# A new hand-written order for everything behind attention in a four-layer kernel, with more idle products on TensorE

## What is computed

```
xn = _layernorm(x, axis=-1)
s = attention_l(xn)
g = _silu(ffn_l(xn))
x = x + s * g
```

## Time and profile before

| what | us |
|---|---|
| median of 3 runs | 993.38 (993.24 to 994.14) |
| the profiled execution | 993.47 |
| its span | 991.7 |
| PE busy, share of the span | 921.9, 93% |
| DVE busy, share of the span | 758.0, 76% |
| phase C begins on PE | 610.4 |

### The profile page before, as it was taken

The page is one execution under the profiler, slowest core; times in us unless marked ns, Lnnn a source line. Parts: engine busy times, 40 slices in busy tenths (PEclk is TensorE's granted clock), DMA queues, the critical chain, the costliest instruction groups (busy, mean ns, idle before and its releaser), DMA issues. The chain is left out here.

```text
span 991.7 us, 21236 instructions
## 1 busy us (share of the span) xinstructions
PE 921.9 (93%) x7847; PEld 496.3 (50%) x7847; DVE 758.0 (76%) x1329; ACT 538.3 (54%) x902; POOL 596.8 (60%) x533
## 2 busy tenths in 40 slices
PE   4899998999999999999999998799999888899997
PEld 2346563233333333333322333699888546488794
DVE  6878788888888888887888825983689999863414
ACT  1255346666676666666665785443266144275453
POOL 3660426888778777887777894124635787652333
PEclk9899999999999999999999999999999999999999
DMA  9463525111110201121011123567851200343562
GB/s 318 152 216 104 149 81 159 47 53 48 34 52 25 61 24 49 34 60 58 22 40 41 32 70 90 169 209 225 261 153 43 91 20 24 93 132 102 145 198 80
DMA packets 93749, 98.24 MB, mean 99 GB/s; under 512 B 23344, under 2 KB 69808, under 8 KB 93392
## 3 DMA queue, kind: packets, MB, share of 16 engines
q1 hardware_dynamic: 88528, 86.39, 28.6%
q0 software_dynamic: 5120, 10.50, 3.7%
HBM read 71.09 MB, written 25.30 MB: 97 GB/s over the span
## 5 line engine op out<-in xcount | busy, mean ns | idle before, releaser
L254 PE MATMUL ps<-ar 64*64 64x512 bf16 (+5 forms) x5312 | 532.8, 445 | 14.6 <-DVE small L276 4.9
L254 PEld LDWEIGHTS ps<-ar 64*64 64x64 bf16 (+2 forms) x5312 | 264.0, 136 | 268.0 <-ACT ar L300 88.6
L300 ACT ACTIVATE ar<-ps 128x1024 f32<-128x1024 f32 (+1 forms) x304 | 285.2, 941 | 112.0 <-PE ps L254 105.2
L276 DVE TENSOR_REDUCE small<-ps 128x2 f32<-128x1024 f32 (+2 forms) x276 | 307.2, 1140 | 50.5 <-PE ps L254 49.1
L263 POOL TENSOR_TENSOR psum_sb<-psum_sb,ar 128x1024 f32<-128x1024 f32 x91 | 215.0, 2362 | 57.3 <-DVE on_sb L263 47.0
L263 POOL TENSOR_TENSOR ar<-ar 128x512 f32<-128x512 f32 (+1 forms) x80 | 79.3, 997 | 47.3 <-DVE ar L276 26.1
L322 POOL DMA_INDIRECT gT<-ysort,rt x48 | 46.5, 968 | 99.6 <-issue 98.0
L263 DVE TENSOR_TENSOR ar<-ps,ar 128x256 f32<-128x256 f32 (+4 forms) x56 | 56.2, 1011 | 47.3 <-PE ps L254 46.2
L263 POOL TENSOR_TENSOR psum_sb<-ar 128x1024 f32<-128x1024 f32 x32 | 75.9, 2373 | 13.3 <-ACT ar L300 11.0
L297 ACT COPY ar<-ps 128x256 f32<-128x256 f32 (+1 forms) x84 | 31.6, 385 | 79.2 <-PE ps L254 48.2
L254 PE MATMUL ps<-wA,xnT 128*128 128x512 f32 (+3 forms) x192 | 57.9, 425 | 5.1 <-DVE ar L263 2.9
(11 more groups left out here) (159 smaller groups left out, 1089.4 us busy)
## 6 DMA issues: line engine op xcount, KB each, us to landing
ar<-in_L_up SPq DMA_DIRECT2D x48, 384.0 KB, 4.0
ar<-in_L_b SPq DMA_DIRECT2D x32, 322.0 KB, 3.4
rec_sb<-lscr SPq DMA_DIRECT2D x64, 128.0 KB
scr<-ar SPq DMA_DIRECT2D x48, 128.0 KB, 2.1
ar<-xsort SPq DMA_DIRECT2D x40, 128.0 KB, 4.3
ysort<-ar SPq DMA_DIRECT2D x40, 128.0 KB, 3.1
ar<-scr SPq DMA_DIRECT2D x32, 128.0 KB
xsort<-xs SPq DMA_DIRECT2D x12, 256.0 KB, 6.5
```

The source lines that it names most:

```text
L254: return self.e.matmul(o, l, r, start=start, stop=stop) if self.e else Nothing()
L276: return self.e.tensor_reduce(o, a, AX.X, op, negate=True) if negate else self.e.tensor_reduce(o, a, AX.X, op)
L300: return self.e.activation(o, a, fn, **kw) if self.e else Nothing()
```

## The change

Only the lists of words change. No stage is written anew, and each stage does the same work.

- `ORDER_A["tensor"]` gets five more words: `busy.6.0.50`, `busy.4.0.51`, `busy.4.0.52`, `busy.3.0.53` and `busy.4.0.54`, which are 21 idle products. The rest of that list stands as it stood.
- `ORDER_C` is replaced on all five engines. The words are the same and come equally often, in another order. Only the idle products differ: nine words with 67 products before, fourteen with 94 now. The order on SP comes from a plan in which its transfers share one line.

One line of the diff for A and the first one for C (the lists go on for some 80 lines):

```diff
-        "ln.0.0 ln.0.1 qk.0.0 route.0 v.7 v.5 v.7 ln.0.3 v.1 ln.0.2 route.0 route.1 v.3 v.11 v.5 qk.0.1 v.11 v.3 v.15 "
...
+        "ln.0.0 ln.0.1 qk.0.0 route.0 v.7 v.5 v.7 busy.6.0.50 ln.0.3 v.1 busy.4.0.51 ln.0.2 route.0 route.1 v.3 v.11 v.5 "
...
 ORDER_C = {
     "tensor": (
-        "tables tables tail0 tables tables tables xturn.2 up.2 xturn.2 up.2 end0.2 xturn.2 tail0 tail0 tail0 busy.9.5.0 "
...
+        "tables tables tables busy.14.5.0 tables tables tail0 tail0 xturn.2 xturn.2 up.2 up.2 up.2 xturn.2 up.2 end0.2 "
```

More of the change, by code:

```diff
@@ L148 @@
     "tensor": (
[24 rows of a table removed]
-    "vector": (
-        "tables position tables tail0 tables tables tables end0.2 tables tables tail0 tail0 tail0 end0.2 tables gated.2 "
[18 rows of a table removed]
-    "scalar": (
[17 rows of a table removed]
[25 rows of a table added]
+    "vector": (
+        "position tables tables tables tables tables tail0 gated.2 tail0 tail0 end0.2 gated.2 tables tables gated.2 "
[18 rows of a table added]
+    "scalar": (
[17 rows of a table added]
     "gpsimd": (
         "clear2 ln.1.2 ln.1.3 route.3 route.3 route.3 route.3 gather.2 gather.2 gather.2 gather.2 gather.2 gather.2 "
[6 rows of a table removed]
[6 rows of a table added]
         "gather.4 gather.4 gather.4 gather.4 gather.4 gather.4 gather.4 gather.5 gather.5 gather.5 gather.5 gather.5 "
```

## The result

The changed kernel takes 997.11 us in the median of 16 runs against 993.31 for the kernel before on the same chips: a ratio of 1.0040, 95% interval 1.0028 to 1.0051. The ratios are taken over all runs and not from the two medians, whose quotient is 1.0038; one run of `a_alone`, of 1080.02 us, is left out of its ratio as slow. It is slower by 0.4%, where 984.0 had been forecast. Its profiled execution took 996.48 us with a span of 994.7, which is 3.0 us more than the span of before.

What follows compares the result with a forecast made beforehand. It took PE as bound in layer 3's expert stage, DVE in the tile stage, and chains at the start behind attention and the end; -1.0 - 9.4 + 0.6 - 3.7 + 4.0 = -9.5 from 993.5 gave 984.0 us, range 978.4 to 994.0.

Steps and rivals of the forecast that it cites:

- Part 1: Idle products in A: they hold the clock up near 25 to 32 us and shorten DVE's wait, -1.0 us.
- Part 2: From attention to layer 2's first tile: real work fills PE's waits and two gathers move behind `ln.2.0`, -9.4 us.
- rival (a): Front: delayed softmax sum or SP's queue keeps PE waiting at `ln.1.3`; start gives little, 989.0 us; chance 0.17.
- The delay of `tail0`: Front: last softmax sum some 3 us later, hidden if `up.2` work fills the time until `ln.1.3`.
- Part 3: Tile stage: DVE sets the pace, PE's slack takes in its added work; only DVE's own growth counts, +0.6 us.
- rival (c): Tile stage: PE becomes the bound as idle products delay DVE, up to +11.8 us, total 995.2 or 997.8; chance 0.09.
- Part 4: First `up.4` to last `down.5`: PE is gapless, work leaving it is full gain, less 0.9 us new waits, -3.7 us.
- Part 5: Behind the last `down.5`: PE's chain with all of `att3.3` outlasts the gathers, +4.0 us, ends +1.2 and +7.0.
- the hand-overs: End of kernel: three passes from PE over DVE or ACT and back, 1.2 us each, 3.5 us in all.
- Rival (d): End of kernel: PE's tail runs at the low clock, 999.4 us if all of it, 989 if a third; chance 0.05.
- three signs of being wrong: First tile under 4 us early; DVE idle over 10 us in the tile stage; or gathers still ending last.

Runs made afterwards that it cites:

- a_alone: Kernel before with only the change's 21 idle products in A added: ratio 1.0018 to the kernel before.
- no_tile_products: Changed kernel without its 72 idle products behind the first tile: ratio 1.0078 to the kernel before.
- c_alone: Changed kernel with the old list in A, so without the 21 idle products there: ratio 1.0052 to the kernel before.
- front_new_a: Kernel before with the change's order from attention to the first tile and the change's idle products in A: ratio 0.9965 to the kernel before.
- front_warm_a: Kernel before with the change's order up to the first tile, eight more idle products in that front, and the change's products in A: ratio 0.9993.
- new_half_products: Changed kernel with half of each group of idle products behind the first tile: ratio 1.0041 to the kernel before.
- front_new: Kernel before with the change's order from attention to the first tile, old order behind it, old A: ratio 0.9968 to the kernel before.
- rec_moved: Changed kernel with one `rec.3` word of DVE's list moved behind the first words of `tile.6` and `tile.7`: ratio 1.0055 to the kernel before.
- x_mid_old: Changed kernel with the old order on all engines between `tile.0` and `tile.8`: ratio 1.0040 to the kernel before.
- new_from_up4: Kernel before with the change's order only from the first `up.4` on PE to the end: ratio 1.0035 to the kernel before.
- old_double_products: Kernel before with each idle product behind the first tile doubled, 72 in place of 36: ratio 1.0042 to the kernel before.

## Why the prediction was wrong, point by point

**Part 1** had -1.0 and got -0.9 ahead of phase C in the profiled execution. One execution of each could not have shown that: phase C begins at 607.9 to 614.3 in the nine kernels with the old A and at 606.9 to 609.7 in the eight with the new one, means 610.1 and 609.1. The clock did not stay up but fell later. It was low for 3.4 us in place of 6.8; with the old A this first fall took 3.4 us in six of nine kernels, and 6.8 or 13.7 in the others, with the new one 3.4 in all eight. The windows of the changed kernel that answer to the earlier trace rows:

```profile
25.00:32.00 7.00, 6.34 (x36) 0.87 0.24 102
32.00:40.00 8.00, 7.52 (x23) 0.90 0.58 182
```

The rule of the Trainium skill (TensorE: Matmul & The Clock Gate, section HAM oscillation — how this bites in real kernels), by which short bursts between waits throw the clock back, had been set aside because the waits of the earlier trace rows had left the clock at 1.00. It deserved more: the clock fell in the changed kernel at 30.2 and at 661.7, and in `no_tile_products` at 662.3, 795.4 and 836.3, the last two in the tile stage. But the trace agrees with that rule only in part. The case that the Trainium skill describes there is a wait for a transfer that is longer than the work ahead of it. Ahead of 661.7 the waits were of 0.65 and 0.84 us, and PE was busy for 2.51 of the 4.0 us around them.

At the end of the kernel nothing of the gain in A could be shown. In four pairs that differ in A alone, the ratio with its products is higher by 0.0018 (`a_alone`), lower by 0.0012 (the changed kernel against `c_alone`), lower by 0.0003 (`front_new_a`) and higher by 0.0039 (`front_warm_a`). They lie on both sides of nothing, so a term of -1.0 us (0.001) cannot be told from them. Only the last pair is clear of its intervals, and it is a loss whose cause is open.

**Part 2** had the direction and half the size. Up to the last `down.2` two terms failed. It came 79.6 us after the start of phase C, not 73.6: PE idled 4.8 us, not 3.0, and its work was 74.8 us in place of 70.6, since the sum had put a fall of the clock at nothing. `c_alone`, whose clock stayed up to there, has 71.7 us of work, 4.9 of idle time and 76.7 in all. With 3.4 us of low clock it is 78.2 to 78.3 in six kernels, with 6.8 it is 79.6 to 79.8 in four. So the fall is the larger term, about 3 us.

It was not what decided the first tile, though, and here the path of the sum was wrong too: gathers do not simply follow the last `down.2`. The first row of `gather.2` in POOL's timeline, in `c_alone`:

```profile
693.22 1.00 POOL L324 DMA_INDIRECT gT<-ysort,rt  x1 [13.23 <-issue]
```

and in the changed kernel:

```profile
692.90 1.00 POOL L323 DMA_INDIRECT gT<-ysort,rt  x1 [11.41 <-issue]
```

Counted from the start of phase C, `c_alone` ended `down.2` at 76.7 and began to gather at 85.3, the changed kernel at 79.6 and 83.5. Between the two stand the stores of the result rows. The last one ahead of the gathers was issued at 80.3 in `c_alone`, behind loads of rows and weights on SP, and landed at 84.5; in the changed kernel 80.1 and 82.8. In `new_half_products`, `down.2` ended at 78.3, a store issued at 79.0 landed at 85.4 and the gathers began at 86.5, and its first tile was the latest of all with the new front. So SP's line, which rival (a) had named for another transfer, has a part in this front; no run moved it alone, and its share is not shown. The delay of `tail0` that I had seen and taken for hidden was there: `ln.1.3` came 32.0 us after the start of phase C, 4.1 later than before. Behind `down.2` the sum was near in this execution: 29.7 us to the first tile where 30.5 follow from the forecast. The change wins 4.3 in the front, and `front_new` shows that this gain is real.

**Part 3** is the largest miss, 6.9 of 12.5 us; with the 5.1 of Part 2 it turned the sign, and neither would have done it alone. The step that failed: "As long as DVE sets the pace, PE's 18 us of slack take this in. I take +0.6". The slack did take the second half of the products in, as `new_half_products` showed. But DVE's own time was not what I had summed. I had taken the durations of before and DVE's idle time of before as given. From the first tile to the end of `route.4` it works 1.9 us more: 2.3 for the meeting with POOL at 777 us, 1.7 less at three places where it had met POOL before, and the rest for `gather.2`, `gated.3` and other words that crossed the borders of the stretch. It idles 2.2 us more, since other words wait in other places. And the list of PE puts 3.4 us more between `route.4` and the first `up.4`, which I had written down as work but not as delay. Two such waits in the changed kernel's DVE timeline, where it reaches a step of a tile and a `gated.3` before ACT has got to it:

```profile
762.73 0.42 DVE L277 TENSOR_REDUCE ar<-ar 128x16 f32<-128x256 f32 x1 [0.64 <-ACT ar L301]
...
764.53 0.55 DVE L264 TENSOR_TENSOR psum_sb<-ar,ps 128x384 f32<-128x384 f32 x1 [0.64 <-ACT ar L301]
```

So rival (c) had the place and 7.5 of its 11.8 us, but the wrong mechanism: it is the order of the real work on DVE and PE, and not the idle products. Which of the moved words makes DVE wait was not found: `rec_moved` and `x_mid_old` each took back a part of the order, and neither became faster.

**Part 4** predicted -3.7 and got -0.5. PE's work fell from 104.1 to 102.0 us, not to 99.3: `att3.3` and `ffn2.3` left, but the same instructions of `up.5`, `xturn.5` and `att3.1` took 1.3 us longer in their new places (most of it in products of the form `ps<-ar 128x128`), and waits of 1.9 us opened where 0.9 had been allowed. The other 1.4 us between 102.0 and 99.3 was not broken down. `new_from_up4`, with 103.6 us, has the same length without the new tile stage ahead of it, so it is this order that does not pay.

**Part 5** had the right mechanism and the dear end of the hand-overs. PE's last stretch in the changed kernel, which answers to the earlier trace rows:

```profile
973.75 1.88 PE L255 MATMUL ps<-xnT,wA 128*128 128x512 f32 x4
...
981.63 7.45 PE L255 MATMUL ps<-ar 128*128 128x512 f32 x22
989.76 0.66 PE L258 MATMUL ps<-cf,acc_sb 128*128 128x128 f32 x4 [0.68 <-ACT acc_sb L298]
```

PE was busy for 15.77 of its last 20.8 us, where I had 15.4 of work, and the only wait of a size was 0.68 us: the hand-overs that I had put at 3.5 were filled by other products of the block. So the end cost 1.3, close to my lower end of +1.2. Rival (d), the low clock in the tail, did not happen: the window's clock was 0.95 because it fell at 992.7, when PE had been done since 990.4.

The range from 978.4 to 994.0 did not hold 997.11, because its upper side rested on +0.6 for Part 3 with no allowance for DVE, although DVE was named as the bound of that stage. Of the three signs of being wrong the first and the third are not met: the first tile came 5.2 us early, and the chain that ended last held PE rows. The second is met only if the stage is counted up to the first `up.4`, where DVE idled 11.6 of 151.4 us; up to 850.9 it is 8.7.

## What to carry to other kernels

A new order of the same work must be summed on the engine that sets the pace, waits included, and not only on the one whose list changes most; here that engine's stretch grew by 4.1 us in a stage where I had its list grow by 0.6. A front that ends in stores and gathers must be summed over the transfers too, and not over the last product. Cut such a change where all engines pass the same event and measure the pieces: the first third of this order was worth 0.3% alone, and the rest took more than twice that back. Idle products in the waits of a stage can be worth their place. Their number alone says little: in the new order half of them did the same as all, and in the old order twice as many cost 3.4 us.

## What the runs showed of the hardware

- Two engines held each other up at some meetings: a DVE addition of two SBUF operands took 2.27 us in place of 0.68 beside POOL's additions, and 2.13 in place of 0.69 at another place when the first was moved; POOL's took up to 1.87 in place of 1.07. Reductions that read one tile kept their 2.27 to 2.29 us beside POOL's additions. The Trainium skill (SBUF — State Buffer, section SBUF: two separate sides) says that such an instruction with two SBUF inputs and a GpSimd instruction that reads SBUF lock one port against each other; the traces agree in the rows above, and the 0.71 us at 792.87 in the kernel before shows that a meeting can also pass without cost.
- Between attention and the last experts the granted clock fell at least once in all profiled executions but those of the kernel before and `old_double_products`, at places that moved from kernel to kernel. In the tile stage both kernels without idle products had 10.2 us at 1.2 GHz, and none of the others more than 3.4.
- With the new front, each 3.4 us of low clock moved the last `down.2` by about 1.5 us (76.7, 78.3 and 79.6 us with none, one and two of them), and the first tile not in step with it.
- The clock also fell inside attention, from a time between 522.3 and 526.7 us on and for 3.4 us, in nine of the 17 profiled executions, the kernel before among them. No experiment here went after that.
